# The gates of a mixture of experts turned once, gelu evaluated twice, and the weight splits on another engine

## The reference, cut to what matters

```python
logits = jnp.einsum('bld,ed->ble', x, gate_weight)
expert_k = B * L * CAPACITY
kth_val = jnp.sort(logits.reshape(-1))[expert_k - 1]
mask = (logits >= kth_val).astype(x.dtype)
gates = logits * mask
h = jax.nn.gelu(jnp.einsum('bld,ehd->bleh', x, w1) + b1, approximate=True)
y = jnp.einsum('bleh,edh->blde', h, w2) + b2.T[None, None]
out = jnp.einsum('blde,ble->bld', y, gates)
```

## Time and profile before

| | us |
|---|---|
| median of 3 runs (1121.58 to 1126.65) | 1125.18 |
| the profiled execution, device time | 1126.08 |
| its span, first to last instruction | 1124.3 |
| PE busy in it | 991.4 (88%) |
| DVE busy | 660.9 (59%) |
| ACT busy | 478.9 (43%) |
| POOL busy | 255.7 (23%) |

### The profile page before, as it was taken

How to read it: one execution, slowest core, us unless ns; L and a number is a source line. 1 busy time by engine, 2 the same in 40 slices (tenths; PEclk the granted TensorE clock), 3 DMA queues, 4 the chain that set the end, 5 groups by cost and what they waited for, 6 DMA issues and landing times.

```text
span 1124.3 us, 18908 instructions
## 1 busy us (share of the span) xinstructions
PE 991.4 (88%) x7314; PEld 917.6 (82%) x7314; DVE 660.9 (59%) x1389; ACT 478.9 (43%) x1351; POOL 255.7 (23%) x214
## 2 busy tenths in 40 slices
PE   5779999998588689999987889899999999999998
PEld 5668888777566668787866788899999999999998
DVE  4765254544898654244454587864857575858553
...
DMA packets 8636, 34.48 MB, mean 31 GB/s; under 512 B 610, under 2 KB 5090, under 8 KB 5220
## 3 DMA queue, kind: packets, MB, share of 16 engines
...
## 4 chain that ended last, share of the span: by engine, by line
PE 34%; issue 33%; DVE 16%; POOL 9%; ACT 6%; DMA 1%; POOLq 0%; SPq 0%; DVEq 0%; ACTq 0%
PE D L477 16%; POOL wslot L426 5%; PE S L477 4%; ACT probs L887 4%; PE O L631 3%; POOL h L320 3%; PE O L477 2%; DVE probsT L1142 2%; PE T L523 2%; PE O L725 2%; PE T L615 2%; DVE hid L1151 1%; DVE xc L1079 1%; PE T L513 1%; DVE negmax L1125 1%
## 5 line engine op out<-in xcount | busy, mean ns | idle before, releaser
L477 PE MATMUL O<-hid,wslot 128*128 128x300 f32 (+1 forms) x1536 | 220.5, 302 | 10.2 <-DVE work L1359 10.2
L477 PEld LDWEIGHTS O<-hid,wslot 128*128 128x128 f32 x1536 | 212.5, 189 | 12.6 <-DVE hid L1342 12.6
L477 PE MATMUL D<-xn,wslot 128*128 128x300 f32 (+3 forms) x1248 | 205.8, 313 | 6.3 <-ACT work L1003 6.2
L1340 DVE CAST hid<-work 128x300 fp32r<-128x300 f32 (+1 forms) x256 | 127.6, 498 | 135.9 <-ACT work L1003 135.2
L477 PE MATMUL S<-xn,wslot 128*128 128x300 f32 (+3 forms) x1248 | 199.6, 309 | 0.0
L477 PEld LDWEIGHTS D<-xn,wslot 128*128 128x128 f32 x1248 | 186.2, 194 | 9.6 <-ACT work L1003 6.4
L477 PEld LDWEIGHTS S<-xn,wslot 128*128 128x128 f32 x1248 | 184.8, 193 | 0.6
L1003 ACT ACTIVATE work<-D,prm 128x300 f32<-128x300 f32 (+1 forms) x128 | 64.3, 509 | 262.2 <-PE D L477 258.4
L1342 DVE TENSOR_TENSOR hid<-work,hid 128x300 fp32r<-128x300 f32 (+1 forms) x256 | 159.3, 622 | 8.8
L444 POOL TENSOR_TENSOR probs<-probs,rsum 111x444 f32<-111x444 f32 (+1 forms) x88 | 79.7, 905 | 319.2 <-DVE rsum L1134 319.2
L887 ACT ACTIVATE probs<-S,negmax 111x111 f32<-111x111 f32 (+1 forms) x240 | 81.0, 361 | 110.7 <-DVE negmax L1125 110.7
...
## 6 DMA issues: line engine op xcount, KB each, us to landing
...
```

What stands on the lines that cost most here:

```text
L477: mm = pe.matmul(psum, a, b, start=(first and k == 0), stop=(k == 3 * n - 1))
L1340: nc.vector.tensor_copy(high, moe_g(s)[:, 0:w]).then_inc(m_high, 1)
```

## The change

There are five edits. (1) `spread_gates` is gone. `turn_gates` transposes the gates of each token group once, by 22 products with 8 output rows, in step 5 and in the midst of its `moe_down`; VectorE keeps them as high and low part in `gateT` (`keep_gates`); `spread_gate` then makes each expert's and chunk's gate by one fp32r product with a column of `pick` (L824 of the new kernel), placed between hidden blocks: after each m of step 6 for experts 1 and 0, and after m = 1, 3, 5, 7 of the steps with c = 1 from expert 2 on. (2) The high part of a hidden block is no longer cast by VectorE: ScalarE evaluates gelu a second time from PSUM, into `hid` (L1046 new). The bank is free after this second evaluation (`m_high`). (3) The low parts of the weight pieces of experts 2 to 7 move from GpSimd to VectorE, in quarters of 512 columns (`low_quarter`, L1428 new), in steps 4 to 27. (4) `moe_out` waits for GpSimd's adds (`h_moe`) only where its buffer has been used before. (5) The tile of ones becomes one column read with a repeat, and `b1r` becomes the first part of `gateT`.

```diff
@@ -99,9 +100,11 @@
         addT = sb("addT", [P, KD, TOK])
-        b1r = sb("b1r", [P, FF], F32R)
-        ones_r = sb("ones_r", [P, CW], F32R)
+        gateT = sb("gateT", [P, NG * GW], F32R)
+        b1r = gateT[:, 0:FF]
+        one_r = sb("one_r", [P, 1], F32R)
         b2u = sb("b2u", [P, KD])
+        pick = sb("pick", [P, E], F32R)
@@ -210,6 +220,7 @@
         NSTART = FIRST_W + 1
+        LATE_W = FIRST_W + 14
@@ -224,6 +235,8 @@
+            if i >= LATE_W:
+                return (dve_split, i - LATE_W + 1)
@@ -324,15 +337,30 @@
             a, w = MCHUNKS[c]
-            pool.wait_ge(gb_act, c + 1)
+            pool.wait_ge(gb_act, PLACE[0, c] + 1)
...
+        GT_BATCH = [range(k, min(k + 4, NG)) for k in range(0, NG, 4)]
+        SPREAD = [(e, c) for e in [1, 0] + list(range(2, E)) for c in range(NC)]
+        PLACE = {ec: i for i, ec in enumerate(SPREAD)}
+        def spread_at(e, c, m):
+            if e == 1 and c == 2:
+                return m
+            return PLACE[e, m // 2] if e >= 2 and c == 1 and m % 2 else None
...
             return vbuf[:, j // 3, j % 3 * CW:(j % 3 + 1) * CW] if j < 6 else probs[:, j - 6, 0:CW]
+        def moe_hid(s, k):
+            j, m, w = s // KH, s % KH, MCHUNKS[s // KH % NC][1]
+            return hid[:, j % 2, k, m * CW:m * CW + w]
@@ -412,7 +440,7 @@
             nc.gpsimd.memset(c_eps[:, :], EPS).then_inc(consts, 1)
-            nc.gpsimd.memset(ones_r[:, :].bitcast(F32), 1.0).then_inc(consts, 1)
+            nc.gpsimd.memset(one_r[:, :].bitcast(F32), 1.0).then_inc(consts, 1)
@@ -458,9 +486,6 @@
                 for c in range(NC):
-                    if c == 0 and e + 1 < E:
-                        for i in (2, 3):
-                            split(FIRST_W + W_MOE + 2 * e + i)
@@ -696,7 +721,7 @@
-                    pe.matmul(BH[s % 4][:, 0:w], b1r[:, m * P:(m + 1) * P], ones_r[:, 0:w], start=True, stop=False)
+                    pe.matmul(BH[s % 4][:, 0:w], b1r[:, m * P:(m + 1) * P], one_r[:, 0:1].to_broadcast([P, w]), start=True, stop=False)
@@ -757,7 +782,7 @@
                     if s >= 4:
-                        pe.wait_ge(m_gelu, s - 3)
+                        pe.wait_ge(m_high, s - 3)
@@ -768,25 +793,36 @@
                         variance(3, 3)
+                    if spread_at(e, c, m) is not None:
+                        spread_gate(spread_at(e, c, m))
...
-            def spread_gates(e):
-                for c, (a, w) in enumerate(MCHUNKS):
-                    j = e * NC + c
-                    if j >= 2:
-                        pe.wait_ge(gb_act, j - 1)
-                    for g in range(a // GW, (a + w - 1) // GW + 1):
-                        lo, hi = max(a, g * GW), min(a + w, (g + 1) * GW)
-                        nt = NTOK[g]
-                        mm = pe.matmul(BT[j % 2][:, lo - a:hi - a],
-                                       gates[0:nt, g * E + e:g * E + e + 1].to_broadcast([nt, P]),
-                                       ident[0:nt, lo - g * GW:hi - g * GW], start=True, stop=True)
-                    mm.then_inc(gb_mm, 1)
+            def turn_gates(b):
+                if b >= 2:
+                    pe.wait_ge(gt_ready, b - 1)
+                for k, g in enumerate(GT_BATCH[b]):
+                    for row in (0, DH):
+                        mm = pe.matmul(BT[b % 2][row:row + E, k * GW:k * GW + TM],
+                                       gates[0:TM, g * E:(g + 1) * E], ident[0:TM, 0:TM],
+                                       start=True, stop=True, skip_group_check=True)
+                mm.then_inc(gt_mm, 1)
+            def spread_gate(i):
+                e, c = SPREAD[i]
+                a, w = MCHUNKS[c]
+                if i == 0:
+                    pe.wait_ge(gt_ready, len(GT_BATCH))
+                    pe.wait_ge(gt_pick, 2)
+                if i >= 2:
+                    pe.wait_ge(gb_act, i - 1)
+                pe.matmul(BT[i % 2][:, 0:w], pick[:, e:e + 1].to_broadcast([P, P]), gateT[:, a:a + w],
+                          start=True, stop=True).then_inc(gb_mm, 1)
@@ -802,6 +838,8 @@
                                    between=(lambda: sum_counts(8 * j + 3 + 2 * dc)) if e == 0 else None)
+                    if j == NC and dc == 0:
+                        turn_gates(2)
@@ -812,9 +850,9 @@
                     pe.wait_ge(gates_ready, 1)
-                    spread_gates(0)
-                if c == 1 and e >= 1:
-                    spread_gates(e)
+                    pe.wait_ge(gt_zero, 1)
+                    turn_gates(0)
+                    turn_gates(1)
@@ -979,13 +1017,13 @@
-            def spread(e):
-                for c, (a, w) in enumerate(MCHUNKS):
-                    j = e * NC + c
-                    act.wait_ge(gb_mm, j + 1)
-                    if e >= 2:
-                        act.wait_ge(m_y, KD * ((e - 2) * NC + c + 1))
-                    nc.scalar.activation(moe_gate(e, c)[:, 0:w], BT[j % 2][:, 0:w], ACT.Copy).then_inc(gb_act, 1)
+            def spread(i):
+                e, c = SPREAD[i]
+                w = MCHUNKS[c][1]
+                act.wait_ge(gb_mm, i + 1)
+                if e >= 2:
+                    act.wait_ge(m_y, KD * ((e - 2) * NC + c + 1))
+                nc.scalar.activation(moe_gate(e, c)[:, 0:w], BT[i % 2][:, 0:w], ACT.Copy).then_inc(gb_act, 1)
@@ -1000,12 +1038,15 @@
                     act.wait_ge(m_hid, s - 3)
+                bias = prm[:, S_B1M + e * KH + m:S_B1M + e * KH + m + 1]
                 nc.scalar.activation(moe_g(s)[:, 0:w], BH[s % 4][:, 0:w], ACT.Gelu_apprx_tanh,
-                                     bias=prm[:, S_B1M + e * KH + m:S_B1M + e * KH + m + 1]).then_inc(m_gelu, 1)
-                if c == 1 and m == KH - 1 and e >= 1:
-                    if e == 1:
-                        spread(0)
-                    spread(e)
+                                     bias=bias).then_inc(m_gelu, 1)
+                if s // KH >= 2:
+                    act.wait_ge(m2_mm, KD * (s // KH - 1))
+                nc.scalar.activation(moe_hid(s, 0), BH[s % 4][:, 0:w], ACT.Gelu_apprx_tanh,
+                                     bias=bias).then_inc(m_high, 1)
+                if spread_at(e, c, m) is not None:
+                    spread(spread_at(e, c, m))
@@ -1030,6 +1071,7 @@
             nc.vector.tensor_copy(gateR[:, 0, :], prm[:, S_GATE:S_END]).then_inc(params, 1)
+            nc.vector.memset(pick[:, :].bitcast(F32), 0.0).then_inc(gt_pick, 1)
@@ -1094,6 +1136,10 @@
                 dve.wait_ge(mats_in, 64)
+                dve.wait_ge(gt_pick, 1)
+                for row in (0, DH):
+                    ins = nc.vector.tensor_copy(pick[row:row + E, :], ident[row:row + E, row:row + E])
+                ins.then_inc(gt_pick, 1)
@@ -1276,6 +1322,8 @@
             dve.wait_ge(o_mm[1], len(PAIRS))
+            nc.vector.memset(gateT[:, :].bitcast(F32), 0.0).then_inc(gt_zero, 1)
+            dve.wait_ge(gt_zero, 1)
@@ -1329,17 +1377,28 @@
-            def moe_split(s):
-                c, m = s // KH % NC, s % KH
-                w = MCHUNKS[c][1]
-                j = s // KH
+            def keep_gates(b):
+                dve.wait_ge(gt_mm, b + 1)
+                n, a = len(GT_BATCH[b]), GT_BATCH[b][0] * GW
+                def tokens(t, rows, a):
+                    return t[rows, a:a + n * GW].rearrange("p (g n) -> p g n", n=GW)[:, :, 0:TM]
+                for row in (0, DH):
+                    rows = slice(row, row + E)
+                    nc.vector.tensor_copy(tokens(gateT, rows, a), tokens(BT[b % 2], rows, 0)).then_inc(gt_high, 1)
+                dve.wait_ge(gt_high, 2 * b + 2)
+                low = tokens(gateT, slice(DH, DH + E), a)
+                nc.vector.tensor_tensor(low, tokens(BT[b % 2], slice(DH, DH + E), 0), low.bitcast(F32),
+                                        ALU.subtract).then_inc(gt_ready, 1)
+            def moe_low(s):
+                w = MCHUNKS[s // KH % NC][1]
                 dve.wait_ge(m_gelu, s + 1)
-                if j >= 2:
-                    dve.wait_ge(m2_mm, KD * (j - 1))
-                high, low = (hid[:, j % 2, k, m * CW:m * CW + w] for k in range(2))
-                nc.vector.tensor_copy(high, moe_g(s)[:, 0:w]).then_inc(m_high, 1)
                 dve.wait_ge(m_high, s + 1)
-                nc.vector.tensor_tensor(low, moe_g(s)[:, 0:w], high.bitcast(F32), ALU.subtract).then_inc(m_hid, 1)
+                nc.vector.tensor_tensor(moe_hid(s, 1), moe_g(s)[:, 0:w], moe_hid(s, 0).bitcast(F32),
+                                        ALU.subtract).then_inc(m_hid, 1)
@@ -1354,16 +1413,30 @@
                     return
-                dve.wait_ge(gb_act, e * NC + c + 1)
-                dve.wait_ge(h_moe, max(j - 3, 1))
+                dve.wait_ge(gb_act, PLACE[e, c] + 1)
+                if j >= KD * NC + 4:
+                    dve.wait_ge(h_moe, j - 3)
...
             steps = [(e, c) for e in range(E) for c in range(NC)]
+            def low_quarter(i, k):
```

(16 more changed lines are left out.)

8 lines of the change are left out of this document (added).

## The result

The changed kernel takes 1098.4 us (median of 4 executions, 1098.0 to 1099.3) where the kernel before took 1123.5 beside it: a ratio of 0.9766, 95% interval 0.975 to 0.9783. A later repetition of the changed kernel gave 1099.2 (1099.0 to 1103.3) and 0.9777 (0.9746 to 0.9807). The forecast was 1107 with a range of 1102 to 1117: the sign was right, the gain of 18 us was one of 25, and the time lies outside the range. The profiled execution took 1099.3 us, its span 1097.5, against 1126.1 and 1124.3 before: 26.8 us less.

A forecast was written before the change was run, and what follows sets the result against it. TensorE, busy 88% of the span, was taken as the bound, with only some 5 us in 58 per expert winnable. Terms summed to -18.0 us, from 1126.1 to 1108.1 profiled, a median of 1107; range 1102 to 1117.

The forecast's parts named there:

- The price of the turn products: Steps 5 and 6: 16 transposing products, two records each at 0.113 us a record, 3.6 us; six more 1.4.
- the later bank at the stage's start: Start of the expert stage: bank 0 is free one gelu later, +0.4 us.
- Experts 2 to 6: Large stage: an expert loses 3.63 us in place of 5.11, with waits left at c = 0 and 1; times five, -7.4.
- Expert 7: No weight pieces to split: 0.56 us of gates in place of about 3.1, -2.5 us.
- Steps 2 and 3: Search steps: without eight casts on VectorE, TensorE's waits of 1.2 us vanish, twice; -2.4 us.
- Step 4: Search step of 22.36 us: GpSimd's split, halt and slow restart go, some waits come; 18.3 us, -4.1.
- Step 1: GpSimd's splits of expert 1 stay; the scaling of the keys is taken as held, so only -0.8 us.
- Steps 5 and 6: Gates' products, an up part and two down parts: 26.4 us in place of 27.8, -1.4.
- Step 7: GpSimd's 16 first products and adds now fall here, holding each subtraction below 0.5 us: no cost, 0.5 us if not.
- Small ones: Bank 0 free later at the stage's start, +0.4 us, and two 8-column copies ahead of the masks, +0.2; together +0.6.
- rival of a pair without overlap: Second gelu costs 0.51 us, a pair 1.02, so ScalarE falls behind TensorE in the large stage: 1128 us; chance 9%.
- rival that all gains return as the wait for `moe_out`: Only the early steps win, since the gates' gain comes back as that wait: 1115 to 1121 us; chance 4%.

The follow-up runs named there:

- before_bank: Kernel before with one wait changed: for the expert stage's fifth block TensorE takes its bank after VectorE's cast, not the gelu; 1121.4 us, ratio 0.9975.
- turn128: Changed kernel with 128 columns of weights in each turn product in place of 8, by repeating one column of gates; 1102.4 us in one execution.

## Why the prediction missed

Two steps of its sum failed. The price of the turn products, 0.113 us a record, was taken from rows with 128 columns of weights and used for 8, which cost 0.051: steps 5 and 6 gained 3.8 us where it had 1.4. And the later bank at the stage's start was put down as a cost of 0.4 us and nothing more, while the longer wait moved the fall of TensorE's clock and saved 3.0 us in the router. The model of the large stage held. Its terms against the profiled executions, forecast and then measured:

- *Experts 2 to 6*: -7.4, and -8.5 (58.39 to 56.70, times five). The step model had the right waits in the right places, and the start of each down part came within 0.06 us but for one, expert 4 with c = 1, 0.36 late. Not each size was right: the wait for bank D was 0.28 where I had 0.59, and c = 2 gained 1.20 where I had the 0.96 of its wait, which makes the 1.1 between the two sums.
- *Expert 7*: -2.5, -2.6. *Steps 2 and 3*: -2.4, -2.0. *Step 4*: -4.1, -4.6, with waits of 1.14 for the count at m = 5, about 0.2 at m = 7 and 0.70 for the first in the down part, where I had 1.5, 0.5 and 1.2. *Step 1*: -0.8, -0.8, since the keys were held as the nearest row said.
- *Steps 5 and 6*: -1.4, -3.8. Here the step "16 transposing products now, as fp32 two records each, at 0.113 a record" failed. The price was of rows with 128 columns of weights and was carried over to 8; the run with 128 columns gives it back (0.109), the one with 64 does not. The 22 products cost 2.3 us, not 5.0. *Step 7* gave 1.0 back, where I had "nothing in a path with 0.9 to spare; 0.5 if not": its down part waited 0.78.
- *Small ones*: +0.6, and -5.4 for all that lies ahead of step 1. The 0.4 for the later bank was paid, and bought 3.0 in the router. That a wait moves where the clock falls was in no step of the sum; only the last section named a fall of the clock, and at another place. Another 2.7 us lie ahead of the stage, which began at 605.1 and 602.4; that is chance, as the two profiles of the kernel before differ there by 2.3, and how much of it is in the medians no run shows.

The sum gave 1108.1 for the profiled execution, which took 1099.3. Of the 8.8 us between them, 3.0 are the router (before_bank shows it), 3.0 the rest ahead of step 1 (2.7 of chance, 0.3 since the added 0.6 showed as 0.2 to 0.3), 2.4 steps 5 and 6 (turn128 gives back 2.2), 1.1 the experts, 0.6 step 4 and expert 7; step 7 and steps 2 and 3 take 1.4 back. The range failed beside the sum: of its unknowns mostly costs above the forecast were given room (a pair at 0.51, late quarters), while a price taken from 128 columns for 8 could only be too high. The rival of a pair without overlap is refuted by the 0.39 in the rows. The rival that all gains return as the wait for `moe_out` did not come about, but the gates edit met it when it stood alone.
